# Mixture of experts: the rows of x turned between products, weights split in halves, gathers issued in mid-tile

## The reference

```python
xt = x.reshape(-1, H)                                   # 4096 x 256
shared = silu(xt @ sg_w.T) * (xt @ su_w.T) @ sd_w.T     # 256 -> 512 -> 256
probs = sigmoid(xt @ router_w.T + routing_bias)         # 8 experts
topk_p, topk_idx = top_k(probs, 2)
topk_p = topk_p / sum(topk_p)
w = zeros((T, E)).at[arange(T)[:, None], topk_idx].add(topk_p)
y = (silu(xt @ wg[e].T) * (xt @ wu[e].T)) @ wd[e].T     # for each expert e
out = shared + sum over e of w[:, e] * y[e]
```

## Time and profile before

| | |
|---|---|
| three runs, median (lowest to highest) | 3015.48 us (3013.34 to 3019.45) |
| the profiled execution | 3013.87 us |
| its span | 3010.7 us |
| mean granted TensorE clock | 0.911 of full |
| busy over the span: TensorE, VectorE, ScalarE, GpSimd | 83%, 63%, 48%, 53% |
| `moee_h_lo` on GpSimd (L2079), 110 times | 149.8 us busy |
| `moee_in_lo` on VectorE (L1950), 40 times | 91.7 us busy |

### The profile page before, as it was taken

The page is one execution under the profiler, slowest core; times in us unless marked ns, Lnnn a source line. Parts: engine busy times, 40 slices in busy tenths (PEclk is TensorE's granted clock), DMA queues, the critical chain, the costliest instruction groups (busy, mean ns, idle before and its releaser), DMA issues. The chain is left out here.

```text
span 3010.7 us, 68328 instructions
## 1 busy us (share of the span) xinstructions
PE 2506.7 (83%) x25416; PEld 2101.6 (70%) x25416; DVE 1911.4 (63%) x3347; ACT 1434.2 (48%) x2243; POOL 1591.5 (53%) x1778
## 2 busy tenths in 40 slices
PE   5999999995799978999999802888877599996998
PEld 4676766764576757999999802777777477765897
DVE  2666666775478862436665565878887267774665
ACT  2566655653466652335555401555554255653332
POOL 3566655664354530776666583445444367763343
PEclk8899999998799996999999955989998699997999
DMA  7555655532777832246666473010000578762111
GB/s 167 128 136 142 148 130 133 137 92 67 189 201 200 206 87 84 92 157 205 205 218 223 163 211 106 19 32 21 31 28 22 145 192 219 197 157 70 53 52 46
DMA packets 253228, 384.90 MB, mean 128 GB/s; under 512 B 54624, under 2 KB 184416, under 8 KB 245472
## 3 DMA queue, kind: packets, MB, share of 16 engines
q1 hardware_dynamic: 232448, 302.85, 37.9%
q0 software_dynamic: 17376, 78.13, 7.8%
q10 hardware_dynamic: 3200, 1.05, 0.2%
HBM read 249.05 MB, written 142.08 MB: 130 GB/s over the span
## 5 line engine op out<-in xcount | busy, mean ns | idle before, releaser
L1225 ACT ACTIVATE self_probs<-self_score_ps 128x768 f32<-128x768 f32 x256 | 207.6, 811 | 216.1 <-PE self_score_ps L1127 213.1
L1433 POOL TENSOR_SCALAR_AFFINE_SELECT self_probs<-self_probs 128x512 f32<-128x512 f32 x256 | 167.7, 656 | 217.0 <-ACT self_probs L1225 214.4
L2079 POOL TENSOR_TENSOR moee_h_lo<-moee_h,moee_h_hi 128x512 fp32r<-128x512 f32 x110 | 149.8, 1362 | 208.7 <-ACT moee_h_hi L1846 207.8
L1354 DVE TENSOR_REDUCE self_neg_max<-self_max_ps 128x2 f32<-128x256 f32 x256 | 108.0, 422 | 226.5 <-PE self_max_ps L1113 225.3
L672 DVE TENSOR_REDUCE cross_neg_max<-cross_max_ps 128x4 f32<-128x1024 f32 x128 | 155.9, 1221 | 69.9 <-PE cross_max_ps L461 68.6
L1950 DVE TENSOR_TENSOR moee_in_lo<-moee_in_raw,moee_in_hi 128x2048 fp32r<-128x2048 f32 x40 | 91.7, 2293 | 134.0 <-ACT moee_in_hi L1814 102.3
L1355 DVE TENSOR_REDUCE self_neg_max<-self_max_ps 128x2 f32<-128x512 f32 x256 | 174.2, 681 | 0.0
L589 ACT ACTIVATE cross_probs<-cross_score_ps 128x1024 f32<-128x1024 f32 x128 | 131.1, 1024 | 89.3 <-PE cross_score_ps L483 89.0
L1846 ACT ACTIVATE moee_h_hi<-moee_h 128x512 fp32r<-128x512 f32 x110 | 69.6, 632 | 187.5 <-DVE moee_h L2001 187.5
L3032 POOL TENSOR_TENSOR ffn_g_lo<-ffn_g_full,ffn_g_hi 128x512 fp32r<-128x512 f32 x64 | 82.4, 1287 | 144.3 <-ACT ffn_g_hi L2933 144.3
L79 PE MATMUL moee_g_ps<-moee_x_hi,moee_in_hi 128*128 128x256 f32 x440 | 131.9, 300 | 25.3 <-DVE moee_x_lo L1989 21.1
(11 more groups left out here) (475 smaller groups left out, 9932.2 us busy)
## 6 DMA issues: line engine op xcount, KB each, us to landing
self_q<-self_q_split SPq DMA_DIRECT2D x48, 512.0 KB, 3.2
self_q_raw<-self_q SPq DMA_DIRECT2D x32, 768.0 KB, 7.8
cross_stacks<-cross_qk SPq DMA_DIRECT2D x64, 384.0 KB, 6.9
causal_stacks<-causal_qk SPq DMA_DIRECT2D x64, 384.0 KB, 7.2
moe_y_tiles<-moee_y SPq DMA_DIRECT2D x55, 256.0 KB, 3.2
x_tiles<-zeros SPq DMA_DIRECT2D x16, 624.0 KB, 4.6
moee_x_t<-x_tiles SPq DMA_DIRECT2D x39, 256.0 KB, 3.2
cross_qk<-cross_k_split SPq DMA_DIRECT2D x16, 512.0 KB
```

The costliest lines, as they stand in the source:

```text
L1225: nc.scalar.activation(probs[g % 4][:, a, :, P:], score_ps[:, :, P:], ACT.Exp, scale=HD ** -0.5).then_inc(prob_ready, 1)
L1433: pool.affine_select(diagonal, diagonal, [[0, 2], [0, 2], [1, P]], ALU.is_ge, zero, base=0, channel_multiplier=-1).then_inc(prob_masked, 1)
L2079: pool.tensor_tensor(h_lo[p][f][:].rearrange("p j s -> p (j s)"), h[f][:], h_hi[p][f][:].bitcast(F32).rearrange("p j s -> p (j s)"), ALU.s ...
```

## The change

- **Scan.** Only four sequences are turned ahead of the tiles (`AHEAD = 4`). Each of the other twelve is turned behind one group of 12 matmuls (g, u or y) of tiles 0, 1 and the first half of 2 (`BETWEEN`), and the router's product of the sequence before it follows. The turned rows of all 16 stay in `xT`; they are what `x_hi` and `x_lo` of the shared tiles are made from, so these tiles have no transposes of their own. The two banks that the scan uses are now `xT_ps` and `y_ps[1]`.
- **Routing.** Its steps begin in the second half of tile 2 and end in tile 6, in place of tiles 0 to 3. ScalarE's exponentials (L1834, L1836) now stand between two `silu`, with a table load before and after them.
- **Shared tiles.** `h_lo` is made by VectorE, from SBUF, in place of GpSimd; GpSimd has only the scatters, from tile 6 on and four in a half.
- **Weights.** `in_hi` and `in_lo` are made in two halves (`half_in`, 4 x 256 columns). The first half comes behind the first half's `h_hi` and `y`, the second in the second half of the tile; `out_hi` comes behind the second `h_hi`.
- **Gathers.** `fetch` stands between the first and the second `h_lo` of the tile.
- Several tables of the routing share memory, and `x_t` lies in `xT`.

```diff
-            for b in range(SCANS):
+            BETWEEN = [(t, f, name) for t in range(3) for f in range(PAIRS) for name in "guy"
+                       if (t or name != "y") and (t, f, name) < (2, 0, "v")]
+            def scan(st, f, name):
+                b = scan_at(st, f, name)
+                if b is not None:
+                    scan_batch(b)
+                    logits(b - 1)
+                    if b == B - 1:
+                        logits(b)
+
+            for b in range(AHEAD):
                 scan_batch(b)
                 if b:
                     logits(b - 1)
-            logits(SCANS - 1)
...
             def expand(st, f):
...
-                    pe.wait_ge(inlo_ready, sets(st))
+                pe.wait_ge(inlo_ready, 2 * sets(st) - 1 + f)
...
                     last.then_inc(gu_done, 1)
+                    scan(st, f, name)
...
             def body(st):
                 for f in range(PAIRS):
-                    if f == 1 and st.has(1):
+                    if f == 1 and fresh(st, 1):
                         transpose_x(st)
                     if st.has(0):
                         expand(st, f)
-                    if f == 0 and shared(st) and st.at(0) == 1:
+                    if f == 0 and shared(st) and st.at(0) == 4:
                         rank_choices()
                     if st.has(-1):
                         contract(st, f)
+                        scan(st, f, "y")
...
             def body(st):                                # ScalarE
                 p = st.parity(0)
                 for f in range(PAIRS):
-                    if f == 0 and fresh(st, 1):
-                        split_in(st)
+                    if f == 0 and shared(st) and st.at(0) == 3:
+                        bound_logits()
...
-                    if f == 1 and fresh(st):
-                        split_out(st)
+                    if f == 1 and fresh(st, 1):
+                        split_in(st, 1)
...
+                        scan(st, f, "u")
+                        scan(st, f, "y")
+                    if f == 0 and fresh(st, 1):
+                        split_in(st, 0)
+                    if f == 1 and fresh(st):
+                        split_out(st)
...
             def body(st):                                # VectorE
                 p = st.parity(0)
-                if fresh(st, 1):
-                    lower_in(buffer(st, 1), sets(st, 1))
                 for f in range(PAIRS):
...
+                    if f == 1 and fresh(st, 1):
+                        lower_in(buffer(st, 1), sets(st, 1), 1)
                     if st.has(0):
...
+                    if f == 0 and fresh(st, 1):
+                        lower_in(buffer(st, 1), sets(st, 1), 0)
                     if f == 1 and fresh(st):
                         lower_out(buffer(st), sets(st))
                     if shared(st) and st.has(0):
                         route(st.at(0), f)
+                        dve.wait_ge(hhi_ready, n + 1)
+                        if st.has(-2):
+                            dve.wait_ge(down_done, n - 2 * PAIRS + 1)
+                        dve.tensor_tensor(h_lo[p][f][:].rearrange("p j s -> p (j s)"), h[f][:],
+                                          h_hi[p][f][:].bitcast(F32).rearrange("p j s -> p (j s)"),
+                                          ALU.subtract).then_inc(shared_hlo_ready, 1)
...
-            FIRST, POINTS = 3, 6
+            FIRST, POINTS = 6, 8
...
             def body(st):                                # GpSimd
                 p = st.parity(0)
-                if fresh(st, 2) or fresh(st, 1):
-                    fetch(st)
                 for f in range(PAIRS):
-                    if st.has(0):
+                    if f == 1 and (fresh(st, 2) or fresh(st, 1)):
+                        fetch(st)
+                    if fresh(st):
                         n = st.at(0) * PAIRS + f
```

137 lines of the change are left out of this document (78 added, 59 removed).

## The result

| | before | after |
|---|---|---|
| median of 20 runs each | 3010.94 us | 3022.66 us |
| ratio after / before, 95% interval | | 1.0042 (1.0030 to 1.0053) |
| the profiled execution (its span) | 3013.87 us (3010.7) | 3025.3 us (3023.2) |

What follows compares the result with a forecast made beforehand. TensorE was taken to bound scan and shared tiles, scatters nearly level, with waits for x_lo in routed tiles. 3013.87 - 12 (tile 16) - 19 (routed tiles) = 2982.9 profiled; the median 1.6 above gave 2985 us, range 2970 to 3018.

Steps and rivals of the forecast that it cites:

- Part 1: Start: first product at 1152.2 instead of 1181.18, tile 3 at 1194.5, with 6 us at half clock.
- rival B: Start: clock stays at half rate in tiles 0 to 2, costing 27 us; 3011.5; chance 0.17, shared with another case.
- Parts 2 and 3: Routing and scatters: first scatter 11.3 us later, scatter steps of 1.30 us, so tile 16 comes 12 us earlier.
- Part 4: Routed tiles: 9.32 us each instead of 9.82, without waits for a landing; 38 tiles give -19 us.
- the links: Routed tiles: VectorE and ScalarE steps chaining one tile to the next, 9.09 us, less 0.5 for overlap.
- the term of the collisions: Routed tiles: VectorE colliding with GpSimd's h_lo and gathers lengthens the chain by 0.4 to 0.8 us.
- Rival C: VectorE and GpSimd take turns: scatter steps stay 1.67, routed tile 10.0 us; together +18, 3033.5; chance 0.13.
- Rival A: Routed tiles: late-landing gathers make ScalarE wait for in_raw, tile stays 9.8; only -12 remains, 3003.5; chance 0.20.

Runs made afterwards that it cites:

- after's second profile: The unchanged kernel after profiled again on another chip: one run, 3031.9 us, tile 16 at 194.0, routed tile 10.03 us.
- the third profile: The unchanged kernel after profiled a third time, on another chip: one run, 3034.6 us, tile 16 at 201.7, routed tile 10.02 us.
- e2: Kernel after with GpSimd's h_lo of routed tiles cut to 8 of 512 columns, remainders not computed: ratio to before 0.9944, routed tile 9.34 us.
- e7: Kernel after with the second h_lo of a routed tile moved behind out_lo: ratio to before 1.0013, routed tile 9.53 us.
- e6: Kernel after with in_hi and in_lo whole again at the routed tile's start, gathers still mid-tile: ratio to before 1.0518, routed tile 13.86 us.
- e13: Kernel after with closer routing steps, second h_lo behind out_lo, in_raw three tiles ahead, one scatter per group of products: ratio to before 0.9966, routed tile 9.46 us.
- e14: e13 with ScalarE's first half of in_hi and out_hi put ahead of h_hi in routed tiles: ratio to before 0.9906, routed tile 9.07 us.
- e5: Kernel after with the gather of out_raw moved behind the second h_lo: ratio to before 0.9989, routed tile 9.63 us.
- e4: Kernel after with h_lo of shared tiles 0 to 5 back on GpSimd: ratio to before 1.0017, tile 16 at 192.2.
- e9: Kernel after with two scan sequences behind each of six groups, routing and first scatter one tile earlier: ratio to before 1.0093, tile 16 at 211.4.

## Why the prediction was wrong, step by step

| step | forecast | measured |
|---|---|---|
| first product of tile 0 | 13.1 | 12.9 |
| tile 3 | 55.4 | 56.9 |
| first scatter | 90.2 | 93.7 |
| a step of the scatters | 1.30 | 1.32 |
| tile 16 (before 199.4) | 187.3 | 193.0 |
| routed tile (before 9.80) | 9.32 | 10.02 |
| tile 54 (before 571.6) | 541.5 | 571.5 |

- **Part 1 was right**, within 1.5 us in this profile, and rival B was not what happened: the clock rose 3.8 us after the first product. In after's second profile it rose after 8.6 us, and tile 3 came at 59.1, 3.7 us late. The forecast had no second fall of the clock in tile 2.
- **Parts 2 and 3** had the mechanism right and the size at half: -6.3 us instead of -12. Of the 5.7 missing, 1.5 were in tiles 0 to 2, 2.0 in the routing, 1.4 in the scatters, 0.8 between the last scatter and tile 16. The 2.0 go with the fall of the clock at 1210: in after's second profile, without it, the routing took 34.9 us, as forecast (34.8). TensorE stood 14.24 us for the forecast 12. Even the half isn't firm: in the third profile, with the stalls, tile 16 came at 201.7, 2 us later than in before.
- **Part 4 failed**, and it decided: -19 forecast, +6.3 measured, 25 us apart. The step was "Some links overlap (-0.5), and collisions ... lengthen it by 0.4 to 0.8". The collisions are 1.20 in each tile: 0.95 in `out_lo`, 0.25 in the first half of `in_lo`. Taken off the 10.02 they leave 8.82 for the links, near the 8.6 of the forecast (9.09 - 0.5); no run shows a tile of 8.82, since e2, without collisions, stops at 9.34. So the links were priced well, and the term of the collisions, 0.4 to 0.8, was too small. The forecast had gone by one gather of 3.03 us and asked what VectorE does to GpSimd; the price was in the other direction, GpSimd's 1.3 us `h_lo` holding a VectorE instruction, every tile at the same place, since all engines turn in one ring. The last tile, where 2.7 us more were lost, stands in no term of the sum.
- **Rival C** named the right place ("the second `h_lo` behind two gathers, which puts the tile at 10.0") and got 0.13. Its other half, scatters of 1.67, did not come: 1.32. The Trainium skill, "SBUF — State Buffer", section "SBUF: two separate sides", says that such a pair excludes each other for an instruction's whole length. The trace agrees (1.09 us from the end of `h_lo` to the end of `out_lo`, which takes 1.22 alone), in the routed tiles; in the shared tiles it agrees in part: of 18 scatters that began inside an `h_lo` or `x_lo` of VectorE ten took longer, eight of them 1.30 to 1.43 us, and eight kept their 0.96 or nearly; the ten in which one of these began kept it all. The place to weigh the rule was the order of both engines in the routed tile, not the shared tiles.
- **Rival A** was wrong for this kernel (one wait of 0.9 us), but near: with `out_lo` freed in e7 ScalarE waits 12 times for `in_raw`, and with whole weights these waits are in every tile (e6).
- **Outside of the stage** I had forecast nothing. By the three profiles each, the stage's end is 4 to 13 us later and the block behind 6 to 9 us longer than before's means; the median of the runs rose by 11.7. So some half of the measured loss lies in a block that the change doesn't touch, and only the stage's half answers the forecast.
- **The range.** The bounds named (first scatter -4/+7, scatter 1.22 to 1.40, tile 9.17 to 9.5) add up to 2970 to 3005, not to 2972 to 2998. The result lies outside of both.

## What to carry to other kernels

When work is moved between two engines, lay both engines' instructions on SBUF side by side over one period of the steady loop, and price each overlap in both directions: if the same pair meets in every period, the whole lock is in the ring. A gather or any other instruction of an in-order queue that is put ahead of a small one moves the small one too, and it may be that one that does the harm. Where an engine waits for another, look first for its own work that could stand in that wait: reordering ScalarE (e13 to e14, 18 us) brought more than any other single edit that leaves no work out (the next is e5, 15 us less than after).

## What the runs showed of the hardware

- GpSimd's 128x512 subtraction beside VectorE's subtraction of two SBUF inputs: the one that starts later ends about one own length after the first has ended (`out_lo` 2.17 us instead of 1.22; `h_lo` 1.69 mean instead of 1.30 in e14; a 128x256 step of the routing 1.50 instead of 0.42 in e4).
- TensorE kept its full clock through 16.6 us with 4 transposes and 4 narrow products behind every 12 matmuls (tile 1 of after); with twice as many the mean was 0.74 (tile 1 of e9).
- TensorE can stand 0.4 to 1.1 us, in groups, with no semaphore to wait for, while GpSimd issues scatters back to back; the same program had it in one profile of three, and all seven profiles with it come from two of the six jobs.
- A block whose instructions did not change took 509 to 520 us, at a mean clock of 0.87 to 0.85.
